# Attention: TensorE adds the two half sums of value rows, GpSimd weighs two rows of four, gathers wait for TensorE

## The reference

```
gather = seg_id[:, :, None] - offsets              # offsets 0..3
k_sel, v_sel = rows of K and V at clip(gather)     # four rows per token
scores = einsum(q, k_sel) * SCALE, masked where gather < 0
probs = softmax(scores over the four)
out = einsum(probs, v_sel)                          # sum of four weighed value rows
x = x + out @ Wo.T
```

## Time and profile before

| | us |
|---|---|
| median of 3 runs | 2349.54 (2347.63 to 2350.33) |
| span of the profiled execution, first to last instruction | 2347.3 |
| what lies around the span (median less span) | about 2.2 |
| busy, whole span: TensorE, VectorE, ScalarE, GpSimd | 2020.4, 1715.7, 1398.2, 670.6 |
| the attention in steady state | about 112 to 602 |

### The profile page before, as it was taken

One profiled execution on the slowest core, in us unless ns is written; L12 is line 12 of the kernel. 1 busy time (PEld: TensorE's weight loads), 2 busy tenths in 40 slices (PEclk: granted clock), 3 DMA queues, 4 the chain that ended last, 5 costly groups with the idle time before them and its releaser, 6 DMA issues.

```text
span 2347.3 us, 25386 instructions
## 1 busy us (share of the span) xinstructions
PE 2020.4 (86%) x9524; PEld 945.0 (40%) x9524; DVE 1715.7 (73%) x1387; ACT 1398.2 (60%) x1599; POOL 670.6 (29%) x662
## 2 busy tenths in 40 slices
PE   5888888888599999999999999999000699999998
PEld 2444444444244444444444444444000344444443
DVE  8799999999634534532499998999899644577641
ACT  4678887887422322322499996676899633366530
POOL 2599999998300000000121110222111000000000
PEclk9999999999799999999999999999555899999999
DMA  7789999998346656743699995787998755555541
GB/s 297 283 314 337 348 337 346 335 350 316 126 181 226 225 207 223 259 148 144 242 378 390 378 369 209 264 320 293 401 419 327 291 229 208 205 201 232 233 152 72
DMA packets 131162, 634.60 MB, mean 270 GB/s; under 512 B 12256, under 2 KB 12768, under 8 KB 91104
## 3 DMA queue, kind: packets, MB, share of 16 engines
q1 hardware_dynamic: 85888, 316.81, 37.0%
q0 software_dynamic: 45152, 316.16, 34.6%
HBM read 430.69 MB, written 202.24 MB: 270 GB/s over the span
## 4 chain that ended last, share of the span: by engine, by line
PE 64%; issue 3%; DVE 3%; ACT 2%; POOL 0%; DVEq 0%; ACTq 0%; POOLq 0%
PE fd_pp L1777 42%; PE fd_pp L1791 21%; ACT ff_ring L1720 1%; DVE ff_sig L1575 1%; DVE ff_h_parts L1559 1%; DVE ff_sq L1497 1%; ACT ff_sig L1707 0%; DVE ff_sq L1566 0%; DVE kept_gate L1568 0%; DVE ff_gin L1510 0%; DVE ff_hq L1549 0%; ACT ff_hq L1632 0%; ACT ff_ring L1746 0%; ACT ff_sig L1736 0%; DVE kept_o_peak L1575 0%
## 5 line engine op out<-in xcount | busy, mean ns | idle before, releaser
L1791 PE MATMUL fd_pp<-ff_down,kept_gate 128*128 128x512 f16 x1536 | 458.9, 381 | 193.1 <-DVE ff_up L1616 193.1
L1777 PE MATMUL fd_pp<-ff_h_parts,kept_gate 128*128 128x512 f16 x2304 | 499.6, 380 | 14.3 <-DVE ff_h_parts L1415 14.3
L1777 PE MATMUL fd_pp<-ff_h_parts,ff_up 128*128 128x512 f16 x2304 | 497.4, 379 | 0.0
L1639 ACT ACTIVATE ff_raw<-fd_pp 128x1024 f32<-128x1024 f32 x192 | 194.3, 1017 | 396.5 <-PE fd_pp L1777 396.5
L1777 PEld LDWEIGHTS fd_pp<-ff_h_parts,kept_gate 128*128 128x128 f16 x2304 | 225.9, 98 | 287.9 <-DVE ff_h_parts L1415 14.7
L1777 PEld LDWEIGHTS fd_pp<-ff_h_parts,ff_up 128*128 128x128 f16 x2304 | 225.4, 98 | 271.8
L1420 DVE TENSOR_REDUCE kept_gate_peak<-ff_raw 128x1 f32<-128x2048 f32 x48 | 109.7, 2285 | 292.9 <-ACT ff_raw L1639 292.9
L1791 PEld LDWEIGHTS fd_pp<-ff_down,kept_gate 128*128 128x128 f16 x1536 | 150.6, 98 | 375.9 <-issue 195.8
L1791 PE MATMUL fd_pp<-ff_down,ff_up 128*128 128x512 f16 x768 | 292.2, 380 | 0.0
L1746 ACT ACTIVATE ff_ring<-ff_hq,kept_g 128x2048 int16<-128x2048 f32 x48 | 96.0, 1999 | 191.1 <-DVE ff_hq L1549 189.7
L790 PE MATMUL at_psO<-kept_wo,at_ahi 128*128 128x512 f16 x512 | 155.5, 386 | 36.2 <-ACT at_alo L277 31.6
(11 more groups left out here) (239 smaller groups left out, 3454.9 us busy)
## 6 DMA issues: line engine op xcount, KB each, us to landing
ff_raw<-up_scratch SPq DMA_DIRECT2D x66, 1024.0 KB, 8.5
gate_scratch<-ff_raw POOLq DMA_DIRECT2D x48, 1024.0 KB, 9.1
ff_gin<-gate_scratch SPq DMA_DIRECT2D x48, 1024.0 KB, 8.7
up_scratch<-ff_raw POOLq DMA_DIRECT2D x48, 1024.0 KB, 7.7
ff_gin<-gate_integers SPq DMA_DIRECT2D x73, 512.0 KB, 5.8
gate_integers<-ff_ring POOLq DMA_DIRECT2D x43, 512.0 KB, 8.7
ff_up<-up_scratch SPq DMA_DIRECT2D x21, 1024.0 KB, 9.5
kept_xs<-in_x SPq DMA_DIRECT2D x32, 512.0 KB, 14.6
```

What stands on the lines that cost most here:

```text
L1639: nc.scalar.activation(raw[:, n % UNITS, h * 2 * BLK:(h + 1) * 2 * BLK], pp[(2 * n + h) % 4][:, :, :].rearrange("p a t -> p (a t)"), ACT.C ...
L1777: mm = nc.tensor.matmul(pp[k % 4][:, h, :], wt[w][:, c, f:f + P], a[:, b % 2, :, c, :], start=(q == 0), stop=(q == len(todo) - 1))
L1791: mm = nc.tensor.matmul(pp[k % 8 // 2][:, k % 2, :], a[b % 2][:, f, t * P:(t + 1) * P], wt[w][:, f, :], start=(q == 0 and i == 0), stop=(q ...
```

## The change

- VectorE's `weigh` takes two value rows (1024 numbers a partition) instead of three (1536).
- GpSimd's `weigh_fourth` becomes `weigh_upper` and takes two rows (1024) instead of one (512). Its addition of the upper onto the lower rows stays. Its second addition, into `att`, is gone, and so is the buffer (`room` keeps its place).
- TensorE transposes both halves from `kv_rows` into the same psA, eight products a tile instead of four, the second four accumulating on the first.
- The buffer of tile t is now free when TensorE has turned it, so the gather of t + 6 waits for `aT` instead of `att`. It is also moved: the even tile's gather stands behind `norms`, the odd tile's at the head of the next step, ahead of `add_up`.
- For the last pair VectorE's `sum_last` becomes `add_last`, without the second addition.

```
-                    values = kv[:, t % KR, 0:W - 1, D:2 * D] ...
+                    values = kv[:, t % KR, 0:2, D:2 * D] ...
...
-                    last = kv[:, t % KR, W - 1, D:2 * D] ...
+                    upper = kv[:, t % KR, 2:4, D:2 * D] ...
...
                     pool.wait_ge(m["last"], t + 1)
                     nc.gpsimd.tensor_tensor(lower, lower, upper, ALU.add).then_inc(m["half"], 1)
-                    pool.wait_ge(m["half"], t + 1)
-                    need(pool, m["aT"], t - 1)
-                    nc.gpsimd.tensor_tensor(att[:, t % 2, :], kv[:, t % KR, 0, D:2 * D], kv[:, t % KR, 1, D:2 * D],
-                                            ALU.add).then_inc(m["att"], 1)
 
                 def gather_next(t):
-                    pool.wait_ge(m["att"], t + 1)
-                    gather(t + KR)
+                    if tile(t) and t + KR < NT:
+                        pool.wait_ge(m["aT"], t + 1)
+                        gather(t + KR)
...
                     if pair(s_ - 1) and s_ < NP:
+                        gather_next(2 * s_ - 3)
                         add_up(2 * s_ - 2)
                         add_up(2 * s_ - 1)
-                        gather_next(2 * s_ - 2)
-                        gather_next(2 * s_ - 1)
                     if s_ > 0 and (pair(s_ - 3) or pair(s_ + 3)):
                         norms(s_)
+                    if pair(s_ - 1) and s_ < NP:
+                        gather_next(2 * s_ - 2)
...
                 def turn_a(t):
-                    pe.wait_ge(m["att"], t + 1)
+                    pe.wait_ge(m["half"], t + 1)
                     need(pe, m["alo"], t)
-                    turn(psA, att[:, t % 2, :]).then_inc(m["aT"], 1)
+                    for j in range(2):
+                        for c in range(DC):
+                            mm = nc.tensor.matmul(psA[:, c, :], kv[:, t % KR, j, D + c * P:D + (c + 1) * P], ident[:, :],
+                                                  is_transpose=True, start=(j == 0 and c == 0), stop=(j == 1 and c == DC - 1),
+                                                  skip_group_check=True)
+                    mm.then_inc(m["aT"], 1)
```

More of the change, by code:

```diff
@@ L160, in opening @@
         xhi, xlo = (r.sb(n, [P, 2, DC, P], F16) for n in ("xhi", "xlo"))
-        att, hn = (r.sb(n, [P, 2, D], F32) for n in ("att", "hn"))
+        r.sb("room", [P, 2, D], F32)
+        hn = r.sb("hn", [P, 2, D], F32)
         hT = r.sb("hT", [P, 4, D], F32)
@@ L187, in opening @@
         rows_in = [r.sem(f"rows_in{i}") for i in range(KR)]
-        m = r.sems("xn xT xhi xrest xlo q prod raw sc top ds ex tot inv pr pv last half att aT ahi arest alo o x1 "
+        m = r.sems("xn xT xhi xrest xlo q prod raw sc top ds ex tot inv pr pv last half aT ahi arest alo o x1 "
                    "nmean ssq ssq_v stat aggr sqe root rstd norm x_nmean x_ssq hn hT hT_sb peak h_red h_all reduced")
@@ L544, in sum_last @@
                                             ALU.add).then_inc(m["half"], 1)
-                    dve.wait_ge(m["half"], t + 1)
-                    dve.wait_ge(m["aT"], t - 1)
-                    nc.vector.tensor_tensor(att[:, t % 2, :], kv[:, t % KR, 0, D:2 * D], kv[:, t % KR, 1, D:2 * D],
-                                            ALU.add).then_inc(m["att"], 1)
                 def last_moments(t):
@@ L608, in _ @@
                         if s_ == NP - 1:
-                            sum_last(a + 1)
+                            add_last(a + 1)
                 h_peak(NP - 5)
@@ L682, in gather, with weigh_upper @@
                                                 element_offset=0).then_inc(rows_in[t % KR], 16)
-                def weigh_fourth(t):
-                    last = kv[:, t % KR, W - 1, D:2 * D].rearrange("p (h e) -> p h e", h=H)
+                def weigh_upper(t):
+                    upper = kv[:, t % KR, 2:4, D:2 * D].rearrange("p w (h e) -> p w h e", h=H)
                     pool.wait_ge(rows_in[t % KR], 16 * (t // KR + 1))
@@ L689, in weigh_fourth @@
                         pool.wait_ge(m["pv"], t // 2 * 2 + 2)
-                    nc.gpsimd.tensor_tensor(last, last, pr[:, t % 2, W - 1].unsqueeze(2).to_broadcast([P, H, HD]),
+                    nc.gpsimd.tensor_tensor(upper, upper, pr[:, t % 2, 2:4].unsqueeze(3).to_broadcast([P, 2, H, HD]),
                                             ALU.mult).then_inc(m["last"], 1)
                 def add_up(t):
-                    weigh_fourth(t)
+                    weigh_upper(t)
                     lower, upper = kv[:, t % KR, 0:2, D:2 * D], kv[:, t % KR, 2:4, D:2 * D]
```

14 lines of the change are left out of this document (7 added, 7 removed).

## The result

The changed kernel takes 2372.89 us (median of 4 runs, 2371.82 to 2373.64), the kernel before in the same session 2349.11 (4 runs, 2347.63 to 2350.33). The ratio is 1.0104, 95% interval 1.0092 to 1.0115: slower by 24 us, as forecast in sign, and 3.0 us beyond the forecast of 2369.9. The profiled execution (2373.64, the slowest of the four) has a span of 2371.9 against 2347.3, +24.6. All of it lies ahead of the feed-forward products: from TensorE's first of them to the end it is 1700.4 us before and 1699.6 after.

A forecast was written before the change was run, and what follows sets the result against it. VectorE's order, with GpSimd sharing the pace, was taken to bound the attention at 16.94 us a pair. 17.6 + 1.8 - 0.5 + 1.5 = +20.4 on a span of 2347.3, with 2.2 around it, gave 2369.9; range 2354 to 2382.

The forecast's parts named there:

- the port: VectorE and GpSimd: a two-SBUF-input VectorE instruction and a large GpSimd one exclude each other; VectorE finishes 0.15 us behind.
- VectorE's part: VectorE in a pair: L525 saves 1.06 us, L574 would start at +14.65; left alone it would need 15.73 a pair.
- The odd tile's turn and the gather behind it: TensorE turns the odd tile at +6.84 us; GpSimd's gather waits for it, so weighing starts at +8.15, 1.7 later than now.
- the 3 to 4 named as a sign: Expected in the trace: GpSimd idle some 3 to 4 us ahead of every second gather, TensorE's psA as the releaser.
- W: Time of GpSimd's weighing of two rows, 1024 numbers with a repeated factor: taken as 1.9 to 2.1 us.
- Where they meet: GpSimd's last addition holds VectorE's L574 or L584, depending on the weighing's length; middle taken, +0.65 us a pair.
- its two branches: Last addition starts before L574 and holds it, pair 17.83 us; or L574 slips in and L584 is caught, 17.35.
- The number of steady pairs, start and tail: Attention: 27 x 0.65 = 17.6 us, steps 2 and 3 +1.8, step 31 -0.5, behind the last pair +1.5.
- the faster one: Attention rival: GpSimd's wait and the port do not bind; -0.5 us a pair, about 2337; chance 0.11.
- the loop of TensorE and ScalarE: Next bound in the attention: needs 16.23 us a pair, 16.4 with the odd tile's new transposes.
- the late gather: Rival: odd gather lands after the 17.6 us it has; at 18.6 in all steps some 29 us more; chance 0.03.
- the two others: Rivals on GpSimd's weighing: 1.47 us gives no change, about 2350, chance 0.06; long as the plain addition, 2384, chance 0.08.

The follow-up runs named there:

- the gather behind both: Changed kernel with the odd tile's gather moved behind both add_up of a step, no longer ahead of them: 2330.32 us, ratio 0.9922.
- three rows and one: Changed kernel with the odd gather between the two add_up, but three rows weighed on VectorE and one on GpSimd: 2342.19 us, ratio 0.9977.
- gather between: Changed kernel with the odd tile's gather moved between the two add_up of a step, no longer ahead of both: 2328.14 us, ratio 0.9914.
- the same, loop shorter: Kernel with the odd gather between the two add_up, without four matmuls (products with xlo) of each even query: 2321.24 us, ratio 0.9885.
- the same, loop longer: Kernel with the odd gather between the two add_up, plus four overwritten matmuls ahead of each even query: 2353.17 us, ratio 1.0025.
- gathers moved alone: Kernel before with only the gathers changed: they wait for aT and stand where the changed kernel has them; 2375.36 us, ratio 1.0115.
- last addition in halves: Changed kernel with GpSimd's odd-tile addition of 1024 numbers cut into two instructions of 512: 2352.08 us, ratio 1.0014.
- weighing alone: Kernel before with only the weighing changed, two rows on VectorE and two on GpSimd: 2352.34 us, ratio 1.0013.
- between, 512 and 512: Kernel with the odd gather between the two add_up, the odd tile's addition cut into two instructions of 512: 2331.69 us, ratio 0.9929.
- between, 768 and 256: Kernel with the odd gather between the two add_up, the odd tile's addition cut into 768 and 256 numbers: 2331.01 us, ratio 0.9924.

## Why the forecast came out as it did

One table tests the step that carried the forecast, VectorE's own order plus what the port holds. Held is L571 above 0.35 and L581 above 0.29 (before: L574 and L584), own is 15.73 with two rows on VectorE and 16.79 with three. Both values of own are also measured, in pairs in which nothing is held: 15.73 with the gather behind both, 16.79 in the last pair of three rows and one. VectorE has no idle time in these pairs, so the sum must come out if nothing else in its order grew; that it does says that nothing else did:

| kernel | own | held | sum | steady pair |
|---|---|---|---|---|
| before | 16.79 | 0.15 | 16.94 | 16.94 |
| after | 15.73 | 1.91 | 17.64 | 17.63 |
| after, the five long pairs | 15.73 | 1.15 + 1.69 | 18.57 | 18.58 |
| gather between | 15.73 | 0.37 | 16.10 | 16.11, two of 16.88 |
| the same, loop shorter | 15.73 | 0.38 | 16.11 | 16.11 |
| the same, loop longer | 15.73 | 1.15 or 1.49 | 16.88 or 17.22 | 16.88 and 17.22 by turns |
| gathers moved alone | 16.79 | 0.06 + 0.62 | 17.47 | 17.46 |
| the same, the five long pairs | 16.79 | 1.72 + 0.62 | 19.13 | 19.13 |
| last addition in halves | 15.73 | 0.81 + 0.54 | 17.08 | 17.09 |
| weighing alone | 15.73 | 0.53 + 0.61 | 16.87 | 16.87 |
| between, 512 and 512 | 15.73 | 0.52 | 16.25 | 16.26 |
| between, 768 and 256 | 15.73 | 0.53 | 16.26 | 16.26 |
| between, three rows and one | 16.79 | 0.02 | 16.81 | 16.81 |

- *VectorE's part*: right. L526 takes 1.07 less a pair, L571 is wanted at 392.31 - 377.66 = +14.65, to the hundredth.
- *The odd tile's turn and the gather behind it*: right. Turned at +6.85 (forecast 6.84), gather at +7.12, weighing at +8.08 (8.15). GpSimd's wait ahead of the gather was 4.92, more than the 3 to 4 named as a sign.
- *W*: 1.93, inside 1.9 to 2.1. The Trainium skill's page "GPSIMD Engine Reference", section 3.1, gives about 2.6 cycles an element for a two-input operation. The prediction's estimate from it was 2.2 to 2.4; for the weighing the trace has 1.91 to 1.93 and decides, while the plain addition of the same size, 2.36 to 2.38, lies inside it.
- *Where they meet*: right, and by the first of its two branches: the last addition starts 0.25 ahead of L571 and holds it. That branch was put at 17.83 and came to 17.64, since the second weighing starts 0.05 before the first addition's record ends instead of 0.08 behind it, and the chain starts 0.07 earlier. The middle that I took between the two branches, +0.65, met +0.69, and that is in part luck: the branch that held had been put at +0.89, which over 25 pairs would have been 5 us too much. The page "SBUF — State Buffer" of the Trainium skill, section "Who interferes with whom", has it that a VectorE instruction with two SBUF inputs and a GpSimd one that reads SBUF block each other. The trace agrees: 2.26 against 0.35 here, and 1.98 against 0.29 for L581 in the long pairs.
- *The number of steady pairs, start and tail*: 25 pairs at 0.69 for 27 at 0.65, so 17.2 for 17.6; the periods ahead of them with the 0.3 up to the first +3.0 for +1.8; the last -1.2 for -0.5, since it fell to VectorE's 15.73 and not to the 16.4 of the loop; behind it +0.9 for +1.5. Together 19.9 for 20.4.
- *Missing*: the falls of TensorE's clock, 5 x 0.95 = 4.7. In the span the forecast was 4.2 short (20.4 for 24.6), which is these 4.7 less the 0.5 by which the rest came out lower; in the median it was 3.0 short. The forecast had the transposes raise TensorE's load and did not ask what TensorE would do while the longer pair kept ScalarE waiting for L581 (1.34 at the exponential where it was 0.71). That this wait brings the falls on is not shown; that they cost time through the gather's wait for TensorE is, by that wait (6.63 in the long pair in place of 4.92) and by the weighing alone.
- *The rivals*: the faster one named the right condition, a last addition that ends by +15.5; moving the gather met it (+15.22) with W unchanged. Its bound, the loop of TensorE and ScalarE, is real and was 0.2 too high, 16.4 for 16.19: I had added the 0.44 of the new transposes to 16.23 almost in full, and the loop came out shorter than 16.23. ScalarE's wait for TensorE at `xlo` is 0.71 with the gather between, where L268 waited 1.04 before, which may be part of it; no run takes this apart. Landings at 8.1 to 12.7 (all gathers from 100 to 500 us of the kernel after) ruled out the late gather, and W at 1.93 the two others.

## What to carry to other kernels

Where VectorE and GpSimd take large operands in SBUF side by side, write the pace as VectorE's own order plus what GpSimd holds of it, and look for the hold in durations (minimum against median of one line), never in idle time. A wait put in front of GpSimd's long work moves all of that work along VectorE's order; ask which VectorE instruction its last end will then meet. Put such a wait at the first place where what it waits for is done anyway: here, one line further down was worth 45 us between two otherwise equal kernels.
